# A decoder layer on one core: weight remainders made by TensorE, and head norms by a ones matrix and GpSimd's power

## The chip, the core and the metric

The kernel runs on one core of a Trainium2 chip. The engines are TensorE (PE, with its weight loads shown apart as PEld), VectorE (DVE), ScalarE (ACT), GpSimd (POOL) and SyncE (SP, which here only issues DMAs). Each has its own instruction queue and works it off in order; they meet only in semaphores. The metric is the device time of one execution in microseconds, the median of the runs.

## What is computed

One decoder layer over 16 sequences of 128 tokens and 256 features, three stages, each added to its input and layer-normed:

```
q = (q@fq1.T + b) * (q@fq2.T + b)   # per head, 16 heads of 16; k alike; v = x@wv.T
o = causal (q k^T) v                # no softmax
o = o * rsqrt(mean(o*o, per head) + 1e-5) * norm_w ;  x = LN(x + o @ wo.T)
y = conv(x1 * ctx) * ctx ...        # long convolution, 8 x 8 channel pairs; x = LN(x + y)
W = LUT[4-bit code] * scale         # gate, up, down: 3 matrices of 256 x 2048
x = LN(x + (gelu(x@Wg.T) * (x@Wu.T)) @ Wd.T)
```

All tensors are fp32. The large products run as three passes of TensorE's faster fp32r type: high x low, low x high, high x high, where high is the value rounded to fp32r and low is the remainder (value minus high).

## The kernel before

The 16 sequences go in four groups (0 to 3) of four, 512 tokens each. Features lie on partitions, tokens along the columns. The feed-forward part (FFN) of a group runs in 16 slots; a slot is a `gate` product, an `up` product and the `down` product of the slot before. Attention and convolution of the next group are cut into stages, and up to three stages are put between the three products of each slot (`slots`, and `last_slots` for group 3). So the program is: preparation; attention and convolution of group 0 alone; then three times FFN of group g-1 together with attention and convolution of group g; then the FFN of group 3 alone. Between them stands a `turn`, which projects q, k and v of the next group. The order is written out by hand and is the same list for all engines: `schedule` calls each engine's function of a stage's name, so an engine that waits in a stage holds everything behind it in its own queue.

The stages that matter here, with the slot in which they stand: eight `score` stages (slots 0 to 3; PE makes q k^T, DVE multiplies by the causal mask at L755, PE multiplies by v), `squares` (slot 4; ACT squares o, L583), `sums` (slot 5; PE sums the squares of each head into 64 columns, L1163), `rms` (slot 5; DVE, eleven small operations of 64 columns each, Newton steps for the reciprocal root, L769 to L786), `wide` (slot 6; ACT spreads 64 to 1024 columns, L589), `factor` (slot 7; PE transposes them, L1177, ACT copies them to SBUF, L596, DVE multiplies o by them, L793), `outproj` (slot 8; PE, L1187), `norm` (slot 9).

In group 0, where no FFN runs beside, the FFN weights are unpacked in 24 pieces of 512 columns: SP fetches codes and scales into one of two buffers, DVE shifts (L718), masks (L729) and scales (L733) them to `weight`, ACT rounds that to `ffn_hi` (L539), and two pieces later DVE subtracts for `ffn_lo` (L724). One piece stands beside each `score` stage. PE has little to do there and runs filler products (`keep_busy`, L1077), eight in each score stage. The last nine pieces go beside the slots of group 1, one each in slots 1 to 9 (`SECOND`).

GpSimd, which has no access to PSUM, makes the pair products of the convolution (L486) and the reciprocal roots of the layer norms as a power of -0.5 over two columns (L436).

Of the kernel before, what the change touches and what calls it, by code (L numbers as in the profile page):

```python
# [20 lines left out]
P = 128  # L21
# [11 lines left out]
NQ = F // QC  # L33
NTOEP = 4
NU_S = KT * NB
LN_EPS = 1e-5
# [16 lines left out]
def decoder_layer(nc, x, xT, ctx, ctxT, wq, wk, wvT, woT, fT, bias, skip, toep,  # L53
# [7 lines left out]
    with ExitStack() as stack:  # L61
# [13 lines left out]
        toep_sb = sb("toep_sb", [P, NTOEP, 2 * P])  # L75
        ident = sb("ident", [P, P])
        causal = sb("causal", [P, P])
        head_one = sb("head_one", [P, HT, DK])
# [5 lines left out]
        skip_sb = sb("skip_sb", [P, 1])  # L84
        minus_half = sb("minus_half", [P, 1])

        with ExitStack() as early:
# [4 lines left out]
            inter = sbe("inter", [P, 2, T])  # L92
        wv_lo = sb("wv_lo", [P, KT, D], F32R)
        xT_lo = sb("xT_lo", [P, KT, T], F32R)
        inter_lo = sb("inter_lo", [P, 2, T], F32R)

        xT_hi = sb("xT_hi", [P, KT, T], F32R)
# [6 lines left out]
        conv_sb = gate_q[:].rearrange("p k (b t) -> p k b t", b=NB)  # L104
        qT_sb = sb("qT_sb", [P, KT, T])
        rms_sb = x1T_sb = qT_sb
# [36 lines left out]
        ffn_banks = psum[4:8]  # L143
        skip_ps = x2T_ps = psum[4:6]


        def sems(*names):
# [3 lines left out]
            "ld_fold", "ld_wo", "ld_factors", "ld_small", "ld_xT", "ld_x", "ld_ctxT", "ld_ctx", "stored")  # L151
        ld_w = sems("ld_w_even", "ld_w_odd")
        ld_toep = sems(*[f"ld_toep{i}" for i in range(NTOEP)])

# [16 lines left out]
            "ms_ready", "newton_step", "rms_ready", "half_ready", "sk_ready", "x2lo_ready", "inter_ready", "ilo_ready")  # L171
        shifted, masked, deq_ready, wlo_ready = sems("shifted", "masked", "deq_ready", "wlo_ready")

        y_ready, st_ready, mv_ready, ve_ready, ln_ready = (
# [6 lines left out]

        last_mm, last_stored = sems("last_mm", "last_stored")
        end_inter, end_hi, end_lo = sems("end_inter", "end_hi", "end_lo")
        rstd_ready = sems("rstd_ready1", "rstd_ready2", "rstd_ready3")


        raw_w = sb("raw_w", [P, 2, QC], I32)
        raw_s = sb("raw_s", [P, 2, QC])
        code = sb("code", [P, 2, QC], I32)
# [61 lines left out]

        SECOND = [(0, 1, 0) if 1 <= s <= 9 else (0, 0, 0) for s in range(NT)]
        START = 1
        FIRST = START + 4 + sum(with_piece(*stage) for slot in slots for stage in slot)
        UNITS_FIRST = FIRST + 2

        def is_last(g):
# [19 lines left out]
        def ahead(g):  # L277

            return g == 1

        def proj_bank(g, p):
# [71 lines left out]
        def _(sp):  # L353
# [24 lines left out]
            def fetch(u):  # L378
                m, c = units[u]
                codes, scales = packed[m]  # L380
                sp.dma_start(raw_w[:, u % 2, :], codes[:, c * QC:(c + 1) * QC]).then_inc(ld_w[u % 2], 16)
                src = scales[:, c * QC:(c + 1) * QC].unsqueeze(1).broadcast_to([HT, P // HT, QC])
                sp.dma_start(raw_s[:, u % 2, :], src).then_inc(ld_w[u % 2], 16)

            fetch(0)
            fetch(1)
            load(0)
            for u in range(2, len(units)):
# [4 lines left out]
                sp.wait_ge(deq_ready, u - 1)  # L393
                fetch(u)
# [13 lines left out]
        def _(pool):  # L408
# [4 lines left out]
            nc.gpsimd.memset(skip_mat[:], 1.0).then_inc(filled, 1)  # L413
            nc.gpsimd.memset(minus_half[:], -0.5).then_inc(filled, 1)
            nc.gpsimd.memset(v_sb[:], 0.0).then_inc(filled, 1)
            pool.wait_ge(filled, 6)
            masks = ((head_one, HT, DK), (skip_mat, CH, CI))
# [83 lines left out]
            def norm2(g, _):  # L501
                rstd(g, 1)

            schedule(pool, turn, {"score": score, "norm": norm, "norm2": norm2, "x1T": x1T, "conv": conv}, nothing, nothing, nothing, nothing,
                     lambda: rstd(G - 1, 2))
# [3 lines left out]
        def _(act):  # L509
# [11 lines left out]
            act.dma_start(wo_sb[:], woT.rearrange("(k p) n -> p k n", p=P)).then_inc(ld_wo, 16)  # L521

            for i in range(4):
# [7 lines left out]
            act.wait_ge(filled, 6)  # L531
            act.wait_ge(bd_ready, 1)

            def unpack(step):
# [140 lines left out]
        def _(dve):  # L675
# [34 lines left out]
            def unpack(n):  # L710
                if n < NU:


                    dve.wait_ge(ld_w[n % 2], 32 * (n // 2 + 1))
                    if n:
                        dve.wait_ge(deq_ready, n)
                    for w in range(2):
                        nc.vector.tensor_scalar(code[:, w], raw_w[:, n % 2], 28 - 4 * w, 3, ALU.logical_shift_left,  # L718
                                                ALU.arith_shift_right).then_inc(shifted, 1)
                q = n - 2  # L720
                if 0 <= q < NU:
                    m, c = units[q]
# [4 lines left out]
                if n < NU:  # L727
                    dve.wait_ge(shifted, 2 * n + 2)
                    nc.vector.tensor_scalar(code[:], code[:], -0x72000000, None, ALU.bitwise_and).then_inc(masked, 1)  # L729
                    if n >= 2:  # L730
                        dve.wait_ge(wlo_ready, n - 1)
                    dve.wait_ge(masked, n + 1)
                    nc.vector.scalar_tensor_tensor(weight[:, n % 2], code_f16, 2.0 ** 14,  # L733
                                                   raw_s[:, n % 2].unsqueeze(1).broadcast_to([P, 2, QC]),
                                                   ALU.mult, ALU.mult).then_inc(deq_ready, 1)
# [321 lines left out]
        def _(pe):  # L1057
# [70 lines left out]
            def score(g, u):  # L1128
# [15 lines left out]
                if u < NU_S:  # L1144
# [10 lines left out]
                    last.then_inc(s_mm, 1)  # L1155
                keep_busy(g, 8 if u < NU_S else 4)

            def sums(g, mt):

                count(pe, sq_ready, 2, g, 2)  # L1160
                for b in range(NB):
# [3 lines left out]
                last.then_inc(ms_mm, 1)  # L1165
                if mt == KT - 1 and ahead(g + 1):
                    for p in range(3):
                        proj(g + 1, p)

            def factor(g, _):  # L1170

                count(pe, wide_ready, 1, g, 1)
                wide = rms_sb[:].rearrange("p k t -> p (k t)")
# [115 lines left out]
            def weights_ready(g, n, m):  # L1289

                if isinstance(g, int) and g == 0 and n % 2 == 0:
                    pe.wait_ge(wlo_ready, 3 * (n // 2) + m)

# [102 lines left out]
```

## Time and profile before

| | |
|---|---|
| median of 3 runs | 555.57 us (554.32 to 555.93) |
| the profiled execution's own time | 556.13 us |
| its span, first to last instruction | 553.8 us |
| PE busy | 529.0 us (96%) |
| DVE busy | 373.8 us (67%) |
| ACT busy | 147.3 us (27%) |
| POOL busy | 124.4 us (22%) |
| mean granted TensorE clock | 0.991 of full |

The busy time of PE counts the filler products too, and its ends are modelled, so whether PE is the limit of a stretch is read from its gaps and from what it waits for. The stretches of the span: preparation and group 0 to 113 us (its scores from 28.4 to 54.5 us), then FFN of group 0 with group 1 to 238.7 us, FFN of group 1 with group 2 to 363.4 us, FFN of group 2 with group 3 to 474 us, FFN of group 3 alone to the end.

### The profile page before, as it was taken

To read this page: it belongs to the slowest core of one execution; us is meant where nothing else is said; L and a number is where in the kernel's file an instruction comes from. 1 tells how busy PE (TensorE), PEld (TensorE's weight loads), DVE (VectorE), ACT (ScalarE), POOL (GpSimd) and SP (SyncE) were. 2 spreads that over 40 slices of the span, in tenths; PEclk is the share of its full clock that TensorE was granted. 3 is DMA by queue.
4 is the path that set the end of the run, shared out by engine and by line. 5 is a ranking of instruction groups with operands and counts; after the bars stand their busy time and mean duration, and the time that the engine had idled before them with its cause. 6 is when DMAs were issued, how large, how long until landed. Compare 5 with 4: busy or idle time off the path is not lost.

```text
span 553.8 us, 8791 instructions
## 1 busy us (share of the span) xinstructions
PE 529.0 (96%) x3351; PEld 430.9 (78%) x3351; DVE 373.8 (67%) x784; ACT 147.3 (27%) x260; POOL 124.4 (22%) x195
## 2 busy tenths in 40 slices
PE   4999889989989999999999999999999999999994
PEld 4766777657878888776888888776888888888883
DVE  3899879967767586975455586976455677753235
ACT  3432320052333112142242112141232111332221
POOL 2100059400002445030002445030003561010001
PEclk9999989989999999999999999999999999999998
DMA  6432223121210110013001111022001120010001
GB/s 190 150 113 80 89 69 96 38 77 40 62 35 30 48 49 29 1 63 130 1 0 30 48 48 30 1 64 92 0 1 44 53 59 0 1 38 2 1 0 38
DMA packets 25257, 26.81 MB, mean 48 GB/s; under 512 B 2816, under 2 KB 22784, under 8 KB 25216
## 3 DMA queue, kind: packets, MB, share of 16 engines
q1 hardware_dynamic: 14208, 15.73, 9.3%
q10 hardware_dynamic: 10576, 8.95, 5.5%
q0 software_dynamic: 432, 1.57, 0.8%
q8 instruction: 26, 0.43, 0.3%
q14 instruction: 15, 0.12, 0.1%
HBM read 24.15 MB, written 2.10 MB: 47 GB/s over the span
## 4 chain that ended last, share of the span: by engine, by line
PE 84%; DVE 8%; DMA 3%; issue 2%; POOL 1%; ACT 1%; ACTq 0%; POOLq 0%; SPq 0%; DVEq 0%
PE bank L1083 17%; PE bank L1085 16%; PE bank L1084 16%; PE front_bank L1215 5%; PE front_bank L1218 5%; PE front_bank L1216 5%; PE front_bank L1152 4%; PE front_bank L1139 3%; PE bank L1077 3%; PE front_bank L1083 2%; PE front_bank L1084 2%; PE front_bank L1085 2%; PE front_bank L1187 2%; DMA wo_sb<-in_woT 1%; PE front_bank L1163 1%
## 5 line engine op out<-in xcount | busy, mean ns | idle before, releaser
L1083 PE MATMUL bank<-x2T_lo,ffn_hi 128*128 128x512 f32 x256 | 110.6, 432 | 1.4 <-DVE x2T_lo L970 1.4
L1027 DVE TENSOR_TENSOR inter<-bank,inter 128x512 f32<-128x512 f32 x63 | 43.5, 690 | 86.1 <-PE bank L1085 85.7
L1085 PE MATMUL bank<-x2T_hi,ffn_hi 128*128 128x512 f32 x256 | 101.6, 397 | 0.0
L1084 PE MATMUL bank<-x2T_hi,ffn_lo 128*128 128x512 f32 x256 | 101.5, 396 | 0.0
L486 POOL TENSOR_TENSOR qbd<-qT_sb,ctxT_sb 128x256 f32<-128x256 f32 x128 | 79.2, 642 | 70.3 <-PE front_bank L1218 56.9
L436 POOL TENSOR_TENSOR ve<-ve,minus_half 128x2 f32<-128x2 f32 x24 | 17.1, 729 | 289.5 <-DVE ve L810 230.5
L667 ACT ACTIVATE inter_hi<-inter 128x512 fp32r<-128x512 f32 x63 | 39.8, 632 | 143.3 <-DVE inter L1027 143.3
L1083 PE MATMUL bank<-ffn_lo,inter_hi 128*128 128x256 f32 x256 | 76.7, 300 | 0.4 <-DVE inter_lo L1008 0.2
L654 ACT ACTIVATE inter<-bank 128x512 f32<-128x512 f32 x64 | 38.2, 598 | 133.7 <-PE bank L1085 133.6
L1085 PE MATMUL bank<-ffn_hi,inter_hi 128*128 128x256 f32 x256 | 71.9, 281 | 0.0
L1084 PE MATMUL bank<-ffn_hi,inter_lo 128*128 128x256 f32 x256 | 71.9, 281 | 0.0
L1016 DVE TENSOR_TENSOR inter_lo<-inter,inter_hi 128x512 fp32r<-128x512 f32 x63 | 47.5, 753 | 23.2 <-PE bank L1085 15.4
L1083 PEld LDWEIGHTS bank<-x2T_lo,ffn_hi 128*128 128x128 f32 x256 | 48.3, 189 | 16.3 <-issue 8.0
L1085 PEld LDWEIGHTS bank<-x2T_hi,ffn_hi 128*128 128x128 f32 x256 | 48.4, 189 | 11.8
L1084 PEld LDWEIGHTS bank<-x2T_hi,ffn_lo 128*128 128x128 f32 x256 | 48.3, 189 | 8.3 <-issue 0.2
L755 DVE TENSOR_TENSOR gate_q<-front_bank,causal 128x1024 f32<-128x1024 f32 x32 | 39.1, 1223 | 21.9 <-PE front_bank L1152 21.9
L1083 PEld LDWEIGHTS bank<-ffn_lo,inter_hi 128*128 128x128 f32 x256 | 48.2, 188 | 5.3 <-issue 3.0
L847 DVE TENSOR_TENSOR qbd<-front_bank,ctxT_sb 128x256 f32<-128x256 f32 x128 | 47.8, 415 | 5.0 <-PE front_bank L1218 4.6
L1084 PEld LDWEIGHTS bank<-ffn_hi,inter_lo 128*128 128x128 f32 x256 | 48.4, 189 | 1.8
L1085 PEld LDWEIGHTS bank<-ffn_hi,inter_hi 128*128 128x128 f32 x256 | 48.2, 188 | 0.0
L852 DVE TENSOR_REDUCE gate_q<-qbd 128x64 f32<-128x512 f32 x64 | 43.9, 686 | 2.2
L1215 PE MATMUL front_bank<-qbd,toep_sb 128*128 128x256 f32 x128 | 39.9, 393 | 2.7 <-POOL qbd L486 1.9
(130 smaller groups left out, 778.9 us busy)
## 6 DMA issues: line engine op xcount, KB each, us to landing
toep_sb<-in_toep ACTq DMA_DIRECT2D x64, 128.0 KB, 2.1
xT_sb<-in_xT SPq DMA_DIRECT2D x4, 512.0 KB, 5.0
ctxT_sb<-in_ctxT SPq DMA_DIRECT2D x4, 512.0 KB, 4.9
x_sb<-in_x SPq DMA_DIRECT2D x4, 512.0 KB, 6.0
ctx_sb<-in_ctx SPq DMA_DIRECT2D x4, 512.0 KB, 6.9
out<-ctxT_sb POOLq DMA_DIRECT2D x3, 512.0 KB, 3.4
raw_w<-in_gate_p SPq DMA_DIRECT2D x8, 128.0 KB
raw_s<-in_gate_s SPq DMA_DIRECT2D x8, 128.0 KB
```

The lines of the kernel that those rows point to most:

```text
L486: nc.gpsimd.tensor_tensor(pairs(kv_sb, h % 2)[:, kt], v_i, c_j, ALU.mult).then_inc(kv_ready, 1)
L654: nc.scalar.activation(inter[:, n % 2, :], gate_ps[:, :], ACT.Gelu_apprx_tanh).then_inc(gelu_ready, 1)
L667: nc.scalar.activation(inter_hi[:, n % 2, :], inter[:, n % 2, :], ACT.Copy).then_inc(ihi_ready, 1)
L755: nc.vector.tensor_tensor(sc_sb.rearrange("p (r k) c -> p r k c", k=2), front_ps[:, :, 0:2 * P].rearrange("p r (k c) -> p r k c", c=P), ca ...
L847: last = nc.vector.tensor_tensor(pairs(z_sb, h % 2)[:, lt], fb[h % 2][:, :].rearrange("p (k b j i) -> p k b j i", k=KT, b=NB, i=CI)[:, lt] ...
L852: nc.vector.tensor_reduce(conv_sb[:, :, :, h * CI:(h + 1) * CI], pairs(z_sb, h % 2), AX.X, ALU.add)\
L1016: nc.vector.tensor_tensor(inter_lo[:, n % 2, :], inter[:, n % 2, :], inter_hi[:, n % 2, :].bitcast(F32), ALU.subtract).then_inc(ilo_ready, 1)
L1027: nc.vector.tensor_tensor(inter[:, n % 2, :], up_ps[:, :], inter[:, n % 2, :], ALU.mult).then_inc(inter_ready, 1)
L1083: nc.tensor.matmul(ps, w_hi, x_lo, start=start, stop=False, skip_group_check=True)
L1084: nc.tensor.matmul(ps, w_lo, x_hi, start=False, stop=False, skip_group_check=True)
L1085: return nc.tensor.matmul(ps, w_hi, x_hi, start=False, stop=stop, skip_group_check=True)
L1215: nc.tensor.matmul(fb[h % 2][:, 0:n], diag, kv[:, 0:n], start=True, stop=True)
```

## The change

Six edits. First, in group 0's eight score stages the remainder `ffn_lo` of one piece (pieces 4 to 11) is made by PE and ACT and not by DVE: PE multiplies `weight` by the identity in plain fp32, runs one filler, and adds `ffn_hi` times minus the identity into the same PSUM bank; ACT copies the bank to `ffn_lo`. This stands in the place of the eight fillers. Second, the piece beside slot 6 of group 1 goes to slot 10. Third, a Gelu activation of one column early in ACT's queue. Fourth, three buffers for the fetched codes and scales, and so three fetches before SP's first other loads. Fifth, in groups 1 to 3 the head norms are made in another way: ACT rounds the squares to a high part, DVE makes the low part, PE multiplies both by a block matrix of ones (16 x 16 blocks), so that each feature's row holds its head's sum, ACT multiplies by 1/16 and adds 1e-5 on the way to `fac_sb`, and GpSimd raises 2 x 512 columns of it to the power -0.5. DVE's eleven operations, ACT's spreading and copies and PE's transposes of these groups go. Sixth, PE's projections of group 1 during `sums` of group 0 wait for ACT's last copy.

```
-        SECOND = [(0, 1, 0) if 1 <= s <= 9 else (0, 0, 0) for s in range(NT)]
+        SECOND = [(0, 1, 0) if 1 <= s <= 10 and s != 6 else (0, 0, 0) for s in range(NT)]
+        def low_on_pe(q):
+            return FIRST_SCORE <= q + 1 < FIRST_SCORE + NU_S
+        def by_block(g):
+            return g > 0
...
-            fetch(0)
-            fetch(1)
+            for u in range(NRAW):
+                fetch(u)
...
+            def wide(g, _):          # POOL
+                if by_block(g):
+                    for mt in range(KT):
+                        count(pool, mean_ready, 2, g - 1, mt + 1)
+                        nc.gpsimd.tensor_tensor(fac_sb[:, mt, :], fac_sb[:, mt, :],
+                                                minus_half[:].broadcast_to([P, T]), ALU.pow).then_inc(fac_ready, 1)
...
+                    if low_on_pe(n):          # ACT, unpack
+                        act.wait_ge(wlo_mm, n + 2 - FIRST_SCORE)
+                        nc.scalar.activation(ffn_lo[:, m, :, c * QC:(c + 1) * QC],
+                                             low_ps[n % 2][:, :].rearrange("p (w n) -> p w n", w=2), ACT.Copy)\
+                            .then_inc(wlo_act, 1)
...
+                if by_block(g):          # ACT, squares
+                    count(act, sq_ready, 2, g, mt + 1)
+                    if mt == 0:
+                        count(act, v_mm, 2, g, 2)
+                    nc.scalar.activation(sq_hi[:, mt, :], rms_sb[:, mt, :], ACT.Copy).then_inc(sqhi_ready, 1)
...
+                if by_block(g):          # ACT, wide
+                    for mt in range(KT):
+                        nc.scalar.activation(by_seq(fac_sb, mt), factor_part(mt), ACT.Identity, scale=1.0 / DK,
+                                             bias=rms_eps[:, 0:1]).then_inc(mean_ready, 1)
+                    return
...
-                if 0 <= q < NU:          # DVE, unpack
+                if 0 <= q < NU and not low_on_pe(q):
...
+                if by_block(g):          # DVE, squares
+                    count(dve, sqhi_ready, 2, g - 1, mt + 1)
+                    nc.vector.tensor_tensor(sq_lo[:, mt, :], rms_sb[:, mt, :], sq_hi[:, mt, :].bitcast(F32),
+                                            ALU.subtract).then_inc(sqlo_ready, 1)
...
-                count(dve, rT_ready, 2, g, 2)          # DVE, factor
+                if by_block(g):
+                    count(dve, fac_ready, 2, g - 1, 2)
+                else:
+                    count(dve, rT_ready, 2, g, 2)
...
-                keep_busy(g, 8 if u < NU_S else 4)          # PE, score
+                if g == 0 and u < NU_S:
+                    low_part(FIRST_SCORE + u - 1)
+                else:
+                    keep_busy(g, 4)
+            def low_part(q):
+                m, c = units[q]
+                pe.wait_ge(deq_ready, q + 1)
+                if q == FIRST_SCORE - 1:
+                    pe.wait_ge(minus_ready, 1)
+                if q >= FIRST_SCORE + 1:
+                    pe.wait_ge(wlo_act, q - FIRST_SCORE)
+                bank = low_ps[q % 2][:, :]
+                nc.tensor.matmul(bank, ident[:], weight[:, q % 2].rearrange("p w n -> p (w n)"),
+                                 start=True, stop=False, skip_group_check=True)
+                keep_busy(0, 1)
+                pe.wait_ge(whi_ready, q + 1)
+                nc.tensor.matmul(bank.rearrange("p (w n) -> p w n", w=2), minus_ident[:],
+                                 ffn_hi[:, m, :, c * QC:(c + 1) * QC], start=False, stop=True,
+                                 skip_group_check=True).then_inc(wlo_mm, 1)
...
+                if by_block(g):          # PE, sums
+                    if g == 1 and mt == 0:
+                        pe.wait_ge(block_ready, 1)
+                    count(pe, sqlo_ready, 2, g - 1, 2)
+                    for b in (2 * mt, 2 * mt + 1):
+                        toks = slice(b * S, (b + 1) * S)
+                        out = fb[b][:, 0:2 * S].rearrange("p (m t) -> p m t", m=KT)
+                        nc.tensor.matmul(out, head_block[:], sq_hi[:, :, toks], start=True, stop=False)
+                        last = nc.tensor.matmul(out, head_block[:], sq_lo[:, :, toks], start=False, stop=True)
+                    last.then_inc(ms_mm, 1)
+                    return
...
+            def factor(g, _):          # PE and ACT
+                if by_block(g):
+                    return
```

PE in group 0, two score stages, before (L1152 is q k^T, L1077 the filler, L1139 the product with v):

```order
L1152 MATMUL front_bank<-qbd,kT_sb 128x256 x4
L1077 MATMUL bank<-fold_hi 128x512 x8
L1139 MATMUL front_bank<-gate_q,v_sb 32x128 x8
L1152 MATMUL front_bank<-qbd,kT_sb 128x256 x4
L1077 MATMUL bank<-fold_hi 128x512 x8
```

The same place in the changed program (L1243 and L1247 are the two identity products):

```order
L1224 MATMUL front_bank<-qbd,kT_sb 128x256 x4
L1243 MATMUL bank<-weight,ident 128x512
L1149 MATMUL bank<-fold_hi 128x512
L1247 MATMUL bank<-ffn_hi,minus_ident 128x512
L1211 MATMUL front_bank<-gate_q,v_sb 32x128 x8
L1224 MATMUL front_bank<-qbd,kT_sb 128x256 x4
```

Seven of the eight fillers of each stage are gone, and one is left between the two identity products.

GpSimd from the end of group 0 to the norm of group 1, before (L442 spreads q for the scores):

```order
L436 TENSOR_TENSOR ve<-ve,minus_half 128x2 x2
L442 TENSOR_TENSOR qbd<-qT_sb,half_sel 128x256 x4
L436 TENSOR_TENSOR ve<-ve,minus_half 128x2 x2
L486 TENSOR_TENSOR qbd<-qT_sb,ctxT_sb 128x256 x28
```

And in the changed program:

```order
L465 TENSOR_TENSOR ve<-ve,minus_half 128x2 x2
L471 TENSOR_TENSOR qbd<-qT_sb,half_sel 128x256 x4
L485 TENSOR_TENSOR kT_sb<-kT_sb,minus_half 128x512 x2
L465 TENSOR_TENSOR ve<-ve,minus_half 128x2 x2
L522 TENSOR_TENSOR qbd<-qT_sb,ctxT_sb 128x256 x28
```

Two powers of 512 columns (`fac_sb` is the tile kT_sb) have come in between the scores and the first norm.

PE in slot 5 of the FFN of group 1, with `sums` of group 2, before:

```order
L1163 MATMUL front_bank<-head_sel,qT_sb 128x8 x4
L1083 MATMUL bank<-x2T_lo,ffn_hi 128x512
L1084 MATMUL bank<-x2T_hi,ffn_lo 128x512
L1085 MATMUL bank<-x2T_hi,ffn_hi 128x512
```

And in the changed program (the tile of the high part is that of xT_hi):

```order
L1261 MATMUL front_bank<-xT_hi,head_block 128x256
L1262 MATMUL front_bank<-sq_lo,head_block 128x256
L1261 MATMUL front_bank<-xT_hi,head_block 128x256
L1262 MATMUL front_bank<-sq_lo,head_block 128x256
L1155 MATMUL bank<-x2T_lo,ffn_hi 128x512
```

Four sums of eight columns have become four of 256 columns, of which two need DVE's low part.

## Rows read from the trace of the kernel before

**Rows 1.** The page: busy us, share of the span and instructions.
```profile
PE 529.0 (96%) x3351; PEld 430.9 (78%) x3351; DVE 373.8 (67%) x784; ACT 147.3 (27%) x260; POOL 124.4 (22%) x195
```

**Rows 2.** Windows: us; PE, PEld, DVE, ACT, POOL busy (count); clock; DMA share; GB/s.
```profile
28.40:54.50 26.10, 26.06 (x257) 16.94 (x257) 24.80 (x48) 6.64 (x14) 1.23 (x2) 1.00 0.34 98
...
113.00:150.00 37.00, 36.89 (x325) 26.21 (x325) 28.06 (x47) 14.81 (x29) 1.53 (x2) 0.95 0.17 54
...
238.70:363.40 124.70, 124.70 (x815) 102.91 (x814) 80.28 (x163) 32.16 (x57) 30.03 (x45) 1.00 0.13 39
```

**Rows 3.** Groups by line and shape, GpSimd: busy us, mean ns, idle before.
```profile
L436 POOL TENSOR_TENSOR ve<-ve,minus_half 128x2 f32<-128x2 f32 x24 | 17.1, 729 | 289.5 <-DVE ve L810 230.5 <-DVE ve L1045 59.0
L463 POOL TENSOR_TENSOR kT_sb<-x_sb,ctx_sb 128x512 f32<-128x512 f32 x8 | 11.1, 1388 | 0.0
L414 POOL MEMSET minus_half<- 128x1 f32 x1 | 0.1, 89 | 0.0
```

**Rows 4.** Line L436 alone: count, shortest, median and longest ns.
```profile
L436 POOL TENSOR_TENSOR ve<-ve,minus_half x24: 690/692/912, 72.5 to 549.6; 128x2 f32<-128x2 f32 x24
```

**Rows 5.** Timeline of group 0's scores, DVE: start, us, engine, line.
```profile
49.08 1.22 DVE L755 TENSOR_TENSOR gate_q<-front_bank,causal 128x1024 f32<-128x1024 f32 x1
...
50.62 0.68 DVE L724 TENSOR_TENSOR ffn_lo<-weight,ffn_hi 128x512 fp32r<-128x512 f32 x1
...
51.22 0.42 DVE L729 TENSOR_SCALAR code<-code 128x512 int32<-128x512 int32 x1
...
52.35 1.22 DVE L755 TENSOR_TENSOR gate_q<-front_bank,causal 128x1024 f32<-128x1024 f32 x1
```

**Rows 6.** The chain of waits: start, us, what; group 0's scores, then group 2.
```profile
47.46 0.57 PE front_bank L1139 x16
48.04 0.64 PE front_bank L1152 x8
48.68 2.04 PE bank L1077 x8
...
289.20 1.73 PE front_bank L1187 x8
...
348.13 1.72 PE bank L1226 x4
```

**Rows 7.** Timeline of group 0's output projection, DVE.
```profile
66.99 0.50 DVE L718 TENSOR_SCALAR code<-raw_w 128x256 int32<-128x256 int32 x2 [0.54 <-DMA raw_s<-in_gate_s]
...
69.14 0.68 DVE L827 TENSOR_TENSOR x_sb<-front_bank,x_sb 128x512 f32<-128x512 f32 x1
```

**Rows 8.** Timeline of group 2's head norm, ACT, PE and DVE.
```profile
270.92 0.28 PE L1083 MATMUL bank<-ffn_lo,inter_hi 128*128 128x256 f32 x1
271.28 0.28 PE L1083 MATMUL bank<-ffn_lo,inter_hi 128*128 128x256 f32 x1
...
272.38 1.07 ACT L583 ACTIVATE qT_sb<-front_bank 128x512 f32<-128x512 f32 x2
...
273.74 0.95 PE L1163 MATMUL front_bank<-head_sel,qT_sb 128*128 128x8 f32 x8
274.55 0.47 PE L1083 MATMUL bank<-x2T_lo,ffn_hi 128*128 128x512 f32 x1
...
282.60 1.04 ACT L589 ACTIVATE qT_sb<-inv_rms 128x1024 f32<-128x1024 f32 x1
283.95 1.03 PE L1177 MATMUL front_bank<-ident,qT_sb 128*128 128x128 f32 x8
284.74 0.48 PE L1083 MATMUL bank<-x2T_lo,ffn_hi 128*128 128x512 f32 x1
...
286.21 1.29 DVE L793 TENSOR_TENSOR gate_q<-front_bank,kT_sb 128x512 f32<-128x512 f32 x2 [2.79 <-ACT kT_sb L596]
```

**Rows 9.** Timeline of group 1's transposes, PE.
```profile
159.21 1.09 PE L1177 MATMUL front_bank<-ident,qT_sb 128*128 128x128 f32 x8 [1.53 <-ACT qT_sb L589]
```

**Rows 10.** Timeline of the preparation, DVE.
```profile
9.86 0.48 DVE L697 TENSOR_SCALAR wo_sb<-wo_sb,b_small 128x512 f32<-128x512 f32 x1 [2.21 <-DMA wo_sb<-in_woT]
```

More of the change, by code:

```diff
@@ L34 @@
 NTOEP = 4
+NRAW = 3
 NU_S = KT * NB
@@ L76, in decoder_layer @@
         ident = sb("ident", [P, P])
+        minus_ident = sb("minus_ident", [P, P], F32R)
         causal = sb("causal", [P, P])
@@ L85, in decoder_layer @@
         minus_half = sb("minus_half", [P, 1])
+        rms_eps = sb("rms_eps", [P, 1])
+        head_block = sb("head_block", [P, P], F32R)
+        warm = sb("warm", [P, 1])
         with ExitStack() as early:
@@ L92, in decoder_layer @@
             inter = sbe("inter", [P, 2, T])
+            qT_sb = sbe("qT_sb", [P, KT, T])
         wv_lo = sb("wv_lo", [P, KT, D], F32R)
@@ L95, in decoder_layer @@
         inter_lo = sb("inter_lo", [P, 2, T], F32R)
+        sq_lo = sb("sq_lo", [P, KT, T], F32R)
         xT_hi = sb("xT_hi", [P, KT, T], F32R)
@@ L104, in decoder_layer @@
         conv_sb = gate_q[:].rearrange("p k (b t) -> p k b t", b=NB)
-        qT_sb = sb("qT_sb", [P, KT, T])
+        sq_hi = xT_hi
         rms_sb = x1T_sb = qT_sb
@@ L143, in decoder_layer @@
         ffn_banks = psum[4:8]
-        skip_ps = x2T_ps = psum[4:6]
+        skip_ps = x2T_ps = low_ps = psum[4:6]
         def sems(*names):
@@ L151, in decoder_layer @@
             "ld_fold", "ld_wo", "ld_factors", "ld_small", "ld_xT", "ld_x", "ld_ctxT", "ld_ctx", "stored")
-        ld_w = sems("ld_w_even", "ld_w_odd")
+        ld_w = sems(*[f"ld_w{i}" for i in range(NRAW)])
         ld_toep = sems(*[f"ld_toep{i}" for i in range(NTOEP)])
@@ L172, in decoder_layer @@
         shifted, masked, deq_ready, wlo_ready = sems("shifted", "masked", "deq_ready", "wlo_ready")
+        minus_ready, wlo_mm, wlo_act = sems("minus_ready", "wlo_mm", "wlo_act")
         y_ready, st_ready, mv_ready, ve_ready, ln_ready = (
@@ L182, in decoder_layer @@
         last_mm, last_stored = sems("last_mm", "last_stored")
+        block_ready, sqhi_ready, sqlo_ready, mean_ready, fac_ready = sems(
+            "block_ready", "sqhi_ready", "sqlo_ready", "mean_ready", "fac_ready")
         end_inter, end_hi, end_lo = sems("end_inter", "end_hi", "end_lo")
         rstd_ready = sems("rstd_ready1", "rstd_ready2", "rstd_ready3")
-        raw_w = sb("raw_w", [P, 2, QC], I32)
-        raw_s = sb("raw_s", [P, 2, QC])
+        raw_w = sb("raw_w", [P, NRAW, QC], I32)
+        raw_s = sb("raw_s", [P, NRAW, QC])
         code = sb("code", [P, 2, QC], I32)
@@ L255, in decoder_layer, with low_parts @@
         UNITS_FIRST = FIRST + 2
+        FIRST_SCORE = START + 4
+        def low_on_pe(q):
+            return FIRST_SCORE <= q + 1 < FIRST_SCORE + NU_S
+        def low_parts(eng, k):
+            beside_scores = sum(low_on_pe(q) for q in range(k))
+            if k > beside_scores:
+                eng.wait_ge(wlo_ready, k - beside_scores)
+            if beside_scores:
+                eng.wait_ge(wlo_act, beside_scores)
         def is_last(g):
@@ L380, in fetch @@
                 codes, scales = packed[m]
-                sp.dma_start(raw_w[:, u % 2, :], codes[:, c * QC:(c + 1) * QC]).then_inc(ld_w[u % 2], 16)
+                sp.dma_start(raw_w[:, u % NRAW, :], codes[:, c * QC:(c + 1) * QC]).then_inc(ld_w[u % NRAW], 16)
                 src = scales[:, c * QC:(c + 1) * QC].unsqueeze(1).broadcast_to([HT, P // HT, QC])
-                sp.dma_start(raw_s[:, u % 2, :], src).then_inc(ld_w[u % 2], 16)
-            fetch(0)
-            fetch(1)
+                sp.dma_start(raw_s[:, u % NRAW, :], src).then_inc(ld_w[u % NRAW], 16)
+            for u in range(NRAW):
+                fetch(u)
             load(0)
-            for u in range(2, len(units)):
+            for u in range(NRAW, len(units)):
                 if u == START + 4 + NU_S // 2:
@@ L392, in _ @@
                     load(1)
-                sp.wait_ge(deq_ready, u - 1)
+                sp.wait_ge(deq_ready, u - NRAW + 1)
                 fetch(u)
@@ L414, in _ @@
             nc.gpsimd.memset(minus_half[:], -0.5).then_inc(filled, 1)
+            nc.gpsimd.memset(rms_eps[:], RMS_EPS).then_inc(filled, 1)
             nc.gpsimd.memset(v_sb[:], 0.0).then_inc(filled, 1)
-            pool.wait_ge(filled, 6)
+            pool.wait_ge(filled, 7)
             masks = ((head_one, HT, DK), (skip_mat, CH, CI))
@@ L502, in norm2 @@
                 rstd(g, 1)
-            schedule(pool, turn, {"score": score, "norm": norm, "norm2": norm2, "x1T": x1T, "conv": conv}, nothing, nothing, nothing, nothing,
+            schedule(pool, turn, {"score": score, "wide": wide, "norm": norm, "norm2": norm2, "x1T": x1T, "conv": conv}, nothing, nothing, nothing, nothing,
                      lambda: rstd(G - 1, 2))
@@ L521, in _ @@
             act.dma_start(wo_sb[:], woT.rearrange("(k p) n -> p k n", p=P)).then_inc(ld_wo, 16)
+            act.wait_ge(filled, 7)
+            nc.scalar.activation(warm[:], minus_half[:], ACT.Gelu_apprx_tanh)
             for i in range(4):
@@ L530, in _ @@
             nc.scalar.activation(wv_hi[:], wv_sb[:], ACT.Copy).then_inc(wvhi_ready, 1)
-            act.wait_ge(filled, 6)
             act.wait_ge(bd_ready, 1)
+            act.wait_ge(const_ready, 4)
+            nc.scalar.activation(head_block[:], head_one[:].rearrange("p h e -> p (h e)"), ACT.Copy)\
+                .then_inc(block_ready, 1)
+            act.wait_ge(const_ready, 4)
+            nc.scalar.activation(minus_ident[:], ident[:], ACT.Copy, scale=-1.0).then_inc(minus_ready, 1)
             def unpack(step):
@@ L711, in unpack @@
                 if n < NU:
-                    dve.wait_ge(ld_w[n % 2], 32 * (n // 2 + 1))
+                    dve.wait_ge(ld_w[n % NRAW], 32 * (n // NRAW + 1))
                     if n:
@@ L730, in unpack @@
                     if n >= 2:
-                        dve.wait_ge(wlo_ready, n - 1)
+                        if low_on_pe(q):
+                            dve.wait_ge(wlo_mm, q + 2 - FIRST_SCORE)
+                        else:
+                            low_parts(dve, n - 1)
                     dve.wait_ge(masked, n + 1)
                     nc.vector.scalar_tensor_tensor(weight[:, n % 2], code_f16, 2.0 ** 14,
-                                                   raw_s[:, n % 2].unsqueeze(1).broadcast_to([P, 2, QC]),
+                                                   raw_s[:, n % NRAW].unsqueeze(1).broadcast_to([P, 2, QC]),
                                                    ALU.mult, ALU.mult).then_inc(deq_ready, 1)
@@ L1155, in score @@
                     last.then_inc(s_mm, 1)
-                keep_busy(g, 8 if u < NU_S else 4)
-            def sums(g, mt):
+                if g == 0 and u < NU_S:
+                    low_part(FIRST_SCORE + u - 1)
+                else:
+                    keep_busy(g, 4)
[14 more added lines that the diff above has]
+                                 skip_group_check=True).then_inc(wlo_mm, 1)
+            def sums(g, mt):
+                if by_block(g):
+                    if g == 1 and mt == 0:
[7 more added lines that the diff above has]
+                    last.then_inc(ms_mm, 1)
+                    return
                 count(pe, sq_ready, 2, g, 2)
@@ L1166, in sums @@
                 if mt == KT - 1 and ahead(g + 1):
+                    pe.wait_ge(wlo_act, NU_S)
                     for p in range(3):
@@ L1170, in factor @@
             def factor(g, _):
+                if by_block(g):
+                    return
                 count(pe, wide_ready, 1, g, 1)
@@ L1291, in weights_ready @@
                 if isinstance(g, int) and g == 0 and n % 2 == 0:
-                    pe.wait_ge(wlo_ready, 3 * (n // 2) + m)
+                    low_parts(pe, 3 * (n // 2) + m)
             def down(g, n, pair_done=None):
```

2 lines of the change are left out of this document (1 added, 1 removed).

## The prediction

> **What bounds the kernel now.** The page comes first: PE is busy for 529 of 553.8 us [rows 1]. The windows then say where that is real. Where FFN and another group run together PE has no gap: in the 124.7 us of the FFN of group 1 it is busy for all of them, while DVE has a third free and POOL three quarters [rows 2]. There, time is PE work, and any new wait of PE is lost in full. In group 0's scores PE is just as busy (26.06 of 26.1 us) [rows 2], but the chain of waits shows 2.04 us of each step going to eight fillers [rows 6], so the limit is elsewhere: on the timeline DVE goes from one mask (49.08) to the next (52.35) without a gap, 3.27 us a step [rows 5]. What matters for the fifth edit is POOL: its only power is over two columns, and it takes 692 ns in the median, with little spread (690 to 912) [rows 4].
>
> All is summed against the profiled execution's own time, 556.13 us (span 553.8 and 2.3 around it), which is 0.56 us above the median of the runs.
>
> **The scores of group 0.** DVE loses the subtraction L724 from each step, 0.60 us from its start to that of the next operation (50.62 to 51.22) [rows 5]: 2.67 us remain. PE's new step is 0.57 (product with v) + 0.64 (q k^T) [rows 6] + the identity product in fp32 + one filler + the second identity product. A 512-column fp32 product costs 1.72 / 2 = 0.86 us (two products of skips, each recorded as two passes) [rows 6]; a filler and the fp32r pass 2.04 / 8 = 0.255 us each. Sum 2.58. The low part waits for `weight`, which DVE finishes as its step ends, and the next mask waits for the q k^T behind it, so the loop passes through both engines: 2.58 and about 0.1 of handing over, 2.7 us. ACT gains one copy of about 0.6 us a step and has the room (6.64 us busy of 26.1) [rows 2]. The first of the eight steps still has the subtraction, so seven shrink by 0.57: **-4.0 us**. Bounds: 0 (if the pass through PE, ACT and PSUM costs as much as it saves) and -4.8 (eight times 0.60).
>
> **The rest of group 0.** One more piece, that beside `rms`, loses its 0.60 us on DVE, and the third buffer takes away a wait of 0.54 us for scales before `outproj` [rows 7], both in front of DVE's addition at 69.14: **-1.0 us** (0 to -1.14). The early Gelu takes a table load out of slot 0, where PE hardly waits at all (36.89 us busy of 37 from 113 on) [rows 2]: 0. The wait of group 1's projections for ACT's last copy: ACT's squares stand behind that copy anyway, 0. The third fetch goes out while `wo` is still arriving, for which DVE waits 2.21 us [rows 10]: **+0.3** (0 to +1).
>
> **Groups 1 to 3, without the power.** In each, PE loses two sums of 0.81 us (273.74 to 274.55) and the transposes, 0.79 us (283.95 to 284.74), and gains eight passes of 256 columns at 0.36 / 3 = 0.12 us (270.92 to 271.28: three such passes), 0.96 us [rows 8]: 1.45 less, **-4.3** in three groups. In group 1 a wait of 1.53 us before the transposes goes too [rows 9]: **-1.5**. DVE's eleven small operations go, but it wasn't late there: 0. Against this stands a new wait: PE's `sums` need ACT's two roundings and DVE's last subtraction. ACT ended the squares at 273.45, 0.29 us before PE wanted them (273.74) [rows 8]. Two more ACT passes of about 0.6 us and one of DVE of 0.65 come in: 1.9 less 0.3 is a wait of 1.6 us each, **+4.8** (bounds +3.3, if the passes overlap, and +6).
>
> Without the power this is -4.0 - 1.0 + 0.3 - 4.3 - 1.5 + 4.8 = **-5.7 us**.
>
> **The power.** Two instructions of 512 columns in each of three groups. What hides them: ACT's work at 282.60 becomes two copies of 0.55, so POOL can start at about 283.25. PE wants `outproj` at 289.20 [rows 6], 0.79 earlier without the transposes, and DVE needs 1.29 us for the factor before [rows 8]: POOL must be done by 287.0. So 3.7 us a group are free; the rest is a wait of DVE, with `inner` of the FFN queued behind it, and so of PE: from `outproj` and the next `up` on PE has nothing that it may do. Nor can the conv stages go ahead, since POOL makes their products behind the powers.
>
> No row has a power of more than two columns, so the price per column is the question.
> - From above: 346 ns, the row of two columns taken as all per column (692 / 2): 354 us a group.
> - From below: 2.7 ns, as POOL's multiplication of 512 columns (1388 ns) [rows 3], with the 692 - 89 = 603 ns of the short power as a cost of each instruction: 2 x (1.39 + 0.60) = 4.0 us a group.
>
> I take it near the upper row: the smallest POOL instruction, a memset of one column, shows that an instruction as such costs about 89 ns [rows 3]; nothing in the trace suggests that a power sets up for longer than a multiplication, so 603 ns belong to two columns, 301 each. 1024 x 0.301 + 0.2 = 309 us a group, of which 3.7 are hidden: 3 x 305.3 = **+916 us**. After each such stand PE may start at the low one of its two clock levels (1.2 and not 2.4 GHz). The one fall inside a full stretch that the rows show is that of 113 to 150 us, granted 0.95 [rows 2], 1.85 us lost: three times, **+5.5**. Forecast: 556.1 - 5.7 + 916 + 5.5 - 0.6 = **1471 us**.
>
> The Trainium skill speaks against so high a price (GPSIMD Engine Reference, Performance versus the Vector engine, and Performance pitfalls): a chain of dependent fp32 operations costs 4 cycles each on that engine, but a loop whose elements are independent is bound by issue, at about 3 operations a cycle, so a short instruction shows the chain and a long one the rate. An estimate by that page: 603 ns are 724 cycles at its 1.2 GHz, 362 a column, some 90 chained operations, at 3 a cycle 30 cycles or 25 ns a column; 26 us a group, and 556.1 - 5.7 + 3 x (25.8 - 3.7) + 5.5 - 0.6 = 622 us. No row shows whether the loop is written so; that is the third line of case 2.
>
> **The cases.** A change within 0.3% (1.7 us) can't be told from none here.
> 1. *Price by the column, 270 to 346 ns* (46%): 1471 us, own range 1370 to 1625. For it: the short power is dear and constant. Against it: there is only one width.
> 2. *Price by blocks of columns or overlapped, 15 to 270 ns* (33%). If the 603 ns pay for a block of four, 151 ns a column, 154 us a group (12%): 555.3 + 3 x 150.7 = 1007 us. A block of eight, 77 us a group (11%): 775 us.
>    If the columns overlap, so that most of 603 ns is the way of one column through the loop, and the pace is that of ten multiplications (10 x 2.7 = 27 ns, 28 us a group; 10%): 555.3 + 3 x 24 = 627 us. For it: two columns are fewer than a loop would take at once. Against it: nothing in the rows.
> 3. *The power is hidden* (17%, of which 14% faster, 3% no change). A fixed cost of 0.6 us per instruction and the pace of a multiplication, 4.0 us against 3.7 free: 556.1 - 5.7 + 0.9 - 0.6 = 551 us, faster. It is the other side, and decides as long as a column costs under about 5 ns, where the wait eats the 5.7 us. For it: POOL has its time free and the 603 ns could be a set-up. Against it: 600 ns of set-up would be seven times the shortest instruction.
> 4. *A few ns a column, 5 to 15* (4%): 552 to 585 us, the gain of the rest lost.
>
> That the first four edits don't do what they say, because PE in the scores waits on the way through ACT, moves every case by up to 5 us and decides only between 3 and no change.
>
> Faster 14%, no change 3%, slower 83%. The range 580 to 1630 us holds cases 1 and 2 and leaves out case 3 and most of case 4; the likeliest case alone spans 1370 to 1625.
>
> **What will show it.** The duration of the two powers of 128x512 in groups 1 to 3: about 154 us each if right, under 2.5 us in case 3. DVE's `factor` waiting for POOL for nearly that pair, PE's windows in slots 7 and 8 empty, and a lower granted clock after them. A score step of 2.7 us for 3.26; PE waiting about 1.6 us for `sq_lo` in each of the three groups; no wait for scales before `outproj` of group 0. I am wrong above all if the power's cost isn't in proportion to its columns; everything else is worth 6 us.

## The result, and the profile after

The changed kernel takes 1040.26 us (median of 4 runs, 1039.70 to 1040.98) against 555.18 us before: a ratio of 1.874 [1.871, 1.877]. It is slower, as forecast, but by 485 us and not by 915.

The page of the changed kernel, busy time of each engine and the shares of its chain of waits by engine, beside [rows 1]:

```profile
PE 529.4 (51%) x3271; PEld 426.1 (41%) x3271; DVE 365.9 (35%) x746; ACT 152.3 (15%) x273; POOL 616.7 (59%) x202
...
POOL 48%; PE 43%; DVE 4%; issue 2%; ACT 1%; DMA 1%; ACTq 0%; POOLq 0%; DVEq 0%
```

PE's busy time is what it was, 529 us, but its share fell from 96 to 51%. POOL has gained 492 us, and POOL makes 48% of the chain. The line that answers to [rows 4] is the power of 512 columns (the changed kernel, that line alone, durations shortest/median/longest in ns):

```profile
L485 POOL TENSOR_TENSOR kT_sb<-kT_sb,minus_half x6: 81911/81920/81949, 155.3 to 808.3; 128x512 f32<-128x512 f32 x6
```

81.92 us an instruction, 160 ns a column, six times with hardly a spread. Who waits for it (the changed kernel's waits: us in total, times, longest):

```profile
DVE gate_q L865 <- POOL kT_sb L485: 491.6, 3, 163.9
...
PE front_bank L1295 <- DVE gate_q L865: 481.3, 4, 160.3
```

DVE stands at `factor` for the whole pair in each group, and PE behind it in `outproj`, 160.3 us at most: of each pair of 163.8 us, 3.6 were hidden (the working had 3.7). The timeline of group 1 in the changed kernel answers to [rows 8], which is of group 2: the roundings and subtractions ahead of `sums`, then the power, `factor` and `outproj`:

```profile
143.74 0.63 ACT L628 ACTIVATE xT_hi<-qT_sb 128x512 fp32r<-128x512 f32 x1
...
144.89 0.63 ACT L628 ACTIVATE xT_hi<-qT_sb 128x512 fp32r<-128x512 f32 x1
...
145.61 0.68 DVE L827 TENSOR_TENSOR sq_lo<-qT_sb,xT_hi 128x512 fp32r<-128x512 f32 x1
...
146.44 0.36 PE L1261 MATMUL front_bank<-xT_hi,head_block 128*128 128x256 f32 x1 [1.79 <-DVE sq_lo L827]
...
155.31 81.93 POOL L485 TENSOR_TENSOR kT_sb<-kT_sb,minus_half 128x512 f32<-128x512 f32 x1 [31.71 <-ACT kT_sb L643]
...
319.23 1.29 DVE L865 TENSOR_TENSOR gate_q<-front_bank,kT_sb 128x512 f32<-128x512 f32 x2 [163.84 <-POOL kT_sb L485]
...
320.57 3.78 PE L1295 MATMUL front_bank<-wo_sb,gate_q 128*128 128x256 f32 x8 [160.26 <-DVE gate_q L865]
323.80 0.99 PE L1155 MATMUL bank<-x2T_lo,ffn_hi 128*128 128x512 f32 x1
```

The new wait of PE for the low parts is there, 1.79 us. In the long wait for the powers the granted clock is 0.52, and after it PE starts at its low clock (granted 0.50, 1.2 GHz): the eight passes of `outproj` take 3.23 us (320.57 to 323.80) where they took 1.73 [rows 6] (windows of the changed kernel; columns as in [rows 2]):

```profile
157.60:319.00 161.40, 2.71 (x18) 2.10 (x16) 0.00 (x0) 0.00 (x0) 161.40 (x2) 0.52 0.00 0
320.57:323.80 3.23, 3.23 (x9) 2.60 (x9) 2.58 (x6) 0.48 (x1) 0.00 (x0) 0.50 0.00 0
```

In group 0 the masks of the score stages, which answer to [rows 5], now alternate between steps of 3.01 and 2.81 us, 2.91 in the mean (the changed kernel's timeline):

```profile
38.79 1.22 DVE L818 TENSOR_TENSOR gate_q<-front_bank,causal 128x1024 f32<-128x1024 f32 x1
...
41.80 1.23 DVE L818 TENSOR_TENSOR gate_q<-front_bank,causal 128x1024 f32<-128x1024 f32 x1
...
44.61 1.22 DVE L818 TENSOR_TENSOR gate_q<-front_bank,causal 128x1024 f32<-128x1024 f32 x1
```

The chain of waits of the same stretch (columns as in [rows 6]; L1243 and L1247 are the identity products, L1149 the filler, L1211 the product with v, L1224 q k^T) goes once through PE and once through DVE in two such steps: 2.87 us from the identity product to the mask (38.93 to 41.80) and 2.95 from the mask to the identity product of the next weight (to 44.75).

```profile
38.93 1.12 PE bank L1243 x2
40.05 0.23 PE bank L1149
40.28 0.23 PE bank L1247
40.52 0.57 PE front_bank L1211 x16
41.09 0.69 PE front_bank L1224 x8
...
41.80 0.04 DVE gate_q L818
...
44.00 0.70 DVE weight L796
...
44.75 1.12 PE bank L1243 x2
```

### The profile page after: what moved, and what is told of

The parts are those of the page before. It is cut to its first block, busy times and chain, and to the rows that moved or that the text cites. A ratio compares the mean times of both kernels' runs of the same rounds, so it can differ in the third digit from the quotient of the medians.

```text
span 1038.2 us, 8626 instructions
## 1 busy us (share of the span) xinstructions
PE 529.4 (51%) x3271; PEld 426.1 (41%) x3271; DVE 365.9 (35%) x746; ACT 152.3 (15%) x273; POOL 616.7 (59%) x202
## 4 chain that ended last, share of the span: by engine, by line
POOL 48%; PE 43%; DVE 4%; issue 2%; ACT 1%; DMA 1%; ACTq 0%; POOLq 0%; DVEq 0%
POOL kT_sb L485 47%; PE bank L1155 8%; PE bank L1156 8%; PE bank L1157 8%; PE front_bank L1323 3%; PE front_bank L1326 2%; PE front_bank L1324 2%; PE front_bank L1295 2%; PE front_bank L1224 2%; PE front_bank L1211 2%; PE front_bank L1155 1%; PE front_bank L1157 1%; PE front_bank L1156 1%; DMA wo_sb<-in_woT 1%; DVE inter L1099 0%
## 5 line engine op out<-in xcount | busy, mean ns | idle before, releaser
L485 POOL TENSOR_TENSOR kT_sb<-kT_sb,minus_half 128x512 f32<-128x512 f32 x6 | 491.5, 81927 | 91.4 <-ACT kT_sb L643 91.4
L1295 PE MATMUL front_bank<-wo_sb,gate_q 128*128 128x256 f32 x64 | 20.7, 483 | 481.3 <-DVE gate_q L865 481.3
L1295 PEld LDWEIGHTS front_bank<-wo_sb,gate_q 128*128 128x128 f32 x64 | 15.1, 242 | 485.8 <-DVE gate_q L865 483.1
L865 DVE TENSOR_TENSOR gate_q<-front_bank,kT_sb 128x512 f32<-128x512 f32 x8 | 5.2, 686 | 492.5 <-POOL kT_sb L485 491.6
```

The source lines that it names most:

```text
L485: nc.gpsimd.tensor_tensor(fac_sb[:, mt, :], fac_sb[:, mt, :], minus_half[:].broadcast_to([P, T]), ALU.pow).then_inc(fac_ready, 1)
L1295: last = nc.tensor.matmul(fb[j][:, (b % 2) * D:(b % 2 + 1) * D], o_sb[:, kt, b * S:(b + 1) * S], wo_sb[:, kt, :], start=kt == 0, stop=kt = ...
```

## The experiments

**The old norms.** The changed kernel without its fifth edit.

```
         def by_block(g):
-            return g > 0
+            return False
```

> The changed kernel with the old head norms in all groups: the identity products, the moved piece, the early Gelu and the third buffer alone. Theory (the power of 1024 columns is the whole loss): the first product of the FFN stood at 110.26 us in the changed kernel and at 113.11 before, and group 1's wait of 1.53 us before its transposes may go since the piece beside slot 6 is moved: 555.2 - 2.9 - 0 to 1.5 = 551 to 552.5 us, faster by 0.5 to 0.8%. Rival (something of these edits also costs in later groups): 555 us or more.

Measured: 550.75 us against 555.21, ratio 0.9919 [0.9902, 0.9936]. Edits one to four and six are a gain of 4.5 us; the whole loss is in the fifth. The transposes of group 1 no longer wait. Of the five edits, the moved piece, the third fetch and the identity products are tried further below; the early Gelu and the wait for ACT's last copy were not run by themselves.

**Times for power.** The same chain of instructions, with the dear operation exchanged for a cheap one (so the reciprocal root is left out of groups 1 to 3).

```
-                                                minus_half[:].broadcast_to([P, T]), ALU.pow).then_inc(fac_ready, 1)
+                                                minus_half[:].broadcast_to([P, T]), ALU.mult).then_inc(fac_ready, 1)
```

> The changed kernel with GpSimd multiplying the 2 x 512 columns by -0.5 in place of raising them to the power -0.5 (the reciprocal root is left out of groups 1 to 3). Theory: two multiplications of 1.39 us fit into the 3.7 us that were reckoned free, so no wait for GpSimd is left; against the kernel with the old norms PE has 4.3 us less work in three groups and waits 5.4 us (three times the 1.79 us seen) for the low parts of the squares: 552 to 553.5 us, within 0.3% of the kernel with the old norms. Rival 1 (the ones matrix is worth its 4.3 us, the wait for the low part overlaps with something): 547 to 549 us. Rival 2 (the free time is shorter than reckoned): 555 us or more, with DVE's factor still waiting for GpSimd.

Measured: 551.68 us, ratio 0.9945 [0.9924, 0.9966]. The price of this one operation, with the low clock that follows its waits, is the difference of 488.6 us between this kernel and the changed one. With the power at a multiplication's cost the fifth edit would still be worth nothing: 0.9 us above the old norms, intervals overlapping. Its work on PE is less, but the wait for the low parts takes the gain back (waits of PE in this kernel):

```profile
PE front_bank L1261 <- DVE sq_lo L827: 5.2, 3, 1.8
```

A multiplication of 512 columns by a broadcast column took 1.04 us, so the pair was hidden.

**Powers of 1 to 128 columns.** The kernel before with a row of scratch instructions ahead of everything.

```
...
+            for op, width in [(ALU.pow, w) for w in (1, 2, 3, 4, 5, 6, 8, 9, 12, 16, 32, 64, 128)] + \
+                             [(ALU.mult, w) for w in (1, 4, 64, 512)]:
+                pool.wait_ge(tried, n)
+                nc.gpsimd.tensor_tensor(power_sb[:, 0:width], base_sb[:, 0:width],
+                                        minus_half[:].broadcast_to([P, width]), op).then_inc(tried, 1)
...
+            nc.gpsimd.tensor_tensor(power_sb[0:16, 0:48], base_sb[0:16, 0:48],
+                                    minus_half[0:16].broadcast_to([16, 48]), ALU.pow).then_inc(tried, 1)
```

> The kernel before, with a row of powers of -0.5 on GpSimd ahead of everything, of 1 to 128 columns, and multiplications of 1, 4, 64 and 512 columns. The power took 692 ns for 2 columns and 81.92 us for 512, which is 160.0 ns a column. Theory A (columns are worked off in fours, about 640 ns a block): 1 to 4 columns 690 ns each, 5, 6 and 8 1330 ns, 9 and 12 1970 ns, 64 columns 10.3 us, 128 columns 20.5 us. Theory B (a set-up of some 370 ns and 160 ns for every column): 1, 2, 3, 4 columns 530, 690, 850, 1010 ns, 8 columns 1650 ns, 64 columns 10.6 us. Theory C (301 ns for each of the first columns, cheaper later): 4 columns about 1290 ns. The time of the kernel is of no use here; it grows by some 55 us.

Groups by line and shape (busy us, mean ns of one); the second one of 128x1 and the one of 128x512 are multiplications, the others powers:

```profile
L438 POOL TENSOR_TENSOR power_sb<-base_sb,minus_half 128x1 f32<-128x1 f32 x1 | 0.7, 666 | 0.1
L438 POOL TENSOR_TENSOR power_sb<-base_sb,minus_half 128x2 f32<-128x2 f32 x1 | 0.7, 706 | 0.1
L438 POOL TENSOR_TENSOR power_sb<-base_sb,minus_half 128x3 f32<-128x3 f32 x1 | 0.9, 877 | 0.1
L438 POOL TENSOR_TENSOR power_sb<-base_sb,minus_half 128x4 f32<-128x4 f32 x1 | 1.0, 1008 | 0.1
L438 POOL TENSOR_TENSOR power_sb<-base_sb,minus_half 128x5 f32<-128x5 f32 x1 | 1.2, 1167 | 0.1
L438 POOL TENSOR_TENSOR power_sb<-base_sb,minus_half 128x8 f32<-128x8 f32 x1 | 1.6, 1635 | 0.1
...
L438 POOL TENSOR_TENSOR power_sb<-base_sb,minus_half 128x128 f32<-128x128 f32 x1 | 20.7, 20727 | 0.1
...
L438 POOL TENSOR_TENSOR power_sb<-base_sb,minus_half 128x1 f32<-128x1 f32 x1 | 0.2, 191 | 0.1
L438 POOL TENSOR_TENSOR power_sb<-base_sb,minus_half 128x512 f32<-128x512 f32 x1 | 1.0, 1042 | 0.1
...
L442 POOL TENSOR_TENSOR power_sb<-base_sb,minus_half 16x48 f32<-16x48 f32 x1 | 8.0, 7986 | 0.1
```

Theory A falls: 3 and 4 columns cost more than 2. Theory B holds from 2 columns on: through 692 ns for 2 and 81920 for 512 columns goes a line of 373 ns and 159.3 ns a column, and it gives 1647 ns for 8 (1635 measured) and 20.76 us for 128 (20.73). One column misses: 666 ns for the 530 of the theory; it was the first power of the run, and whether that or the width is the reason was not tried. In this run the widths of 9 to 64 lay 0.2 to 0.5 us above the line; why was not tried either (64 columns in the next kernel lie on it). All bases here are 2.0, in the changed kernel they are means of squares, and one line fits both; the exponent was -0.5 throughout.

**A power of 64 columns.** The old norms, with the reciprocal root of the 64 distinct head sums on GpSimd in groups 1 to 3.

```
+            def rms(g, _):          # POOL
+                if g > 0:
+                    count(pool, ms_ready, 1, g, 1)
+                    count(pool, wide_ready, 1, g, 0)
+                    nc.gpsimd.tensor_tensor(inv_rms[:], mean_sq[:], minus_half[:].broadcast_to([P, NB * H]),
+                                            ALU.pow).then_inc(rms_ready, 1)
...
```

> The kernel with the old norms, but in groups 1 to 3 the reciprocal root of the 64 head sums is one power of 64 columns on GpSimd in place of DVE's ten Newton steps. Theory (160 ns for each column, whatever the width): 10.3 us a group, from 278.5 to 288.8 us in the place of group 2, where the transposes of PE were due at 283.95 and ACT spreads 1.1 us before: PE waits about 6 us in each group, +18 us, 569 to 572 us. Rival (mostly a set-up, 0.7 to 2 us for 64 columns): hidden, as the kernel with the old norms.

Measured: 576.69 us (572.79 to 578.38), ratio 1.0378 [1.0344, 1.0412], some 5 us above the theory's 569 to 572; the mechanism is as expected. Line and waits of this kernel:

```profile
L485 POOL TENSOR_TENSOR inv_rms<-mean_sq,minus_half x3: 10527/10542/10543, 149.2 to 411.5; 128x64 f32<-128x64 f32 x3
...
PE front_bank L1296 <- ACT qT_sb L654: 18.3, 3, 6.1
```

10.54 us is on the line (10.57), and PE waits 6.1 us in each group. 18.3 us of the 25.9 above the old norms are this wait. Most of the other 7.6 is the low clock after it (window from the transposes of group 1 on, columns as in [rows 2]):

```profile
160.88:165.90 5.02, 5.02 (x18) 4.44 (x19) 1.82 (x5) 2.04 (x4) 0.00 (x0) 0.51 0.01 3
```

From the transposes to `outproj` PE took 7.41, 7.32 and 7.63 us in the three groups and 5.10 with the old norms, which makes 7.1 us more in all.

**The piece put back.** The old norms, with `SECOND` as before.

```
-        SECOND = [(0, 1, 0) if 1 <= s <= 10 and s != 6 else (0, 0, 0) for s in range(NT)]
+        SECOND = [(0, 1, 0) if 1 <= s <= 9 else (0, 0, 0) for s in range(NT)]
```

> The kernel with the old norms (550.75 us), with the moved piece put back beside slot 6 of group 1. Theory: it was this piece, and not the Newton steps, that made PE wait 1.53 us before the transposes of group 1, since the old norms no longer have that wait with the piece moved: about 552.2 us, with a wait of about 1.5 us before the transposes of group 1. Rival (the wait went for another reason, as the third buffer): 550.8 us, no wait.

Measured: 551.46 us, ratio 0.9930 [0.9911, 0.9947]; the interval overlaps that of the old norms. The trace decides: the wait of [rows 9] is back (timeline):

```profile
155.27 1.09 PE L1285 MATMUL front_bank<-ident,qT_sb 128*128 128x128 f32 x8 [1.52 <-ACT qT_sb L647]
```

**The third fetch later.**

```
-            for u in range(NRAW):
+            for u in range(2):
                 fetch(u)
             load(0)
+            fetch(2)
```

> The kernel with the old norms, with the third fetch of codes and scales issued behind SP's first other loads and not ahead of them. Theory: the third fetch shares the DMA engines with wo, for which DVE waits at the start (wo landed 1.1 us later than before in the changed kernel, and the scores began 0.5 us later): 0.3 to 0.6 us faster, 550.2 to 550.5 us, wo again about 7 us under way. Rival (the early Gelu or the longer preparation of constants delays the start): 550.7 us, the scores begin as late as before.

Measured: 550.43 us, ratio 0.9909 [0.9891, 0.9927], not to be told from the old norms. `wo` was under way for 7.43 us here, 7.21 with the old norms and 8.11 in the changed kernel, which issue the same DMAs ahead of it; before it was 6.97. Single profiles scatter as widely as the effect sought, so whether the third fetch delays the start stays open.

**No filler.** The old norms, without `keep_busy(0, 1)` in `low_part`.

> The kernel with the old norms, without the one filler between the two identity products. Theory: the score steps of 2.91 us are set by a loop through DVE and PE (weight, identity products, product with v, q k^T, mask, weight), so 0.25 us less on PE shortens each of seven steps until DVE's own 2.67 us are met: -1.6 us, about 549.2 us. Rival (the filler lies in the time in which the second identity product waits for ACT's rounding): no change, 550.7 us. A lower granted clock in or after the scores would speak for the filler.

Measured: 549.42 us, ratio 0.9900 [0.9877, 0.9923]; the steps are 2.80 us, not the 2.67 expected, and DVE has no gap in them. The expectation of -1.6 us is met with -1.3, but the interval overlaps that of the old norms; that the steps fell is the trace's word.

**The older piece.** Each score stage makes the low part of the piece one older.

```
         def low_on_pe(q):
-            return FIRST_SCORE <= q + 1 < FIRST_SCORE + NU_S
+            return FIRST_SCORE <= q + 2 < FIRST_SCORE + NU_S
...
-                    low_part(FIRST_SCORE + u - 1)
+                    low_part(FIRST_SCORE + u - 2)
...
```

> The kernel with the old norms, where each score stage makes the low part of the piece one older (pieces 3 to 10 for 4 to 11): its weight is finished a whole step before PE wants it. Theory: the wait for the weight is what ties PE to DVE, so without it the step falls from 2.91 us to DVE's own 2.67 us or PE's 2.6: seven steps of 0.24, -1.7 us; one piece less of DVE's work is saved behind the scores and one more ahead of them: about 549 us. Rival (the handing over is somewhere else, as from q k^T to the mask): 550.7 us and steps of 2.9 us.

Measured: 549.19 us, ratio 0.9889 [0.9871, 0.9908], the lowest median of all. The steps are 2.79 us, and DVE has no gap in them (timeline of one step):

```profile
37.61 1.22 DVE L820 TENSOR_TENSOR gate_q<-front_bank,causal 128x1024 f32<-128x1024 f32 x1
38.74 0.49 DVE L780 TENSOR_SCALAR code<-raw_w 128x256 int32<-128x256 int32 x2
39.26 0.43 DVE L791 TENSOR_SCALAR code<-code 128x512 int32<-128x512 int32 x1
39.80 0.69 DVE L798 SCALAR_TENSOR_TENSOR weight<-code,raw_s 128x512 f32<-128x512 f16 x1
40.40 1.22 DVE L820 TENSOR_TENSOR gate_q<-front_bank,causal 128x1024 f32<-128x1024 f32 x1
```

So DVE's own step is 2.79 and not 2.67 us: the shift, which now stands right before the operation that needs it (which waits for the shift's semaphore), takes 0.52 to the next start (38.74 to 39.26) and not 0.41, as it did before the subtraction at 50.62 [rows 5] (the kernel before):

```profile
50.21 0.48 DVE L718 TENSOR_SCALAR code<-raw_w 128x256 int32<-128x256 int32 x2
```

**All three.** The older piece, the later fetch, no filler.

> The kernel with the old norms, with all three: the low part of the piece one older, no filler between the identity products, and the third fetch behind SP's first other loads. Theory: with the older piece the score step is DVE's own 2.79 us (mask 1.13, shift 0.52, and 0.53, scale 0.61), so the missing filler gives nothing more there (PE waits instead), and the late fetch moved nothing that can be told from the scatter of wo's arrival (7.0 to 8.1 us over all runs): as the kernel with the older piece, 549 us. Rival (PE's and DVE's steps are so near each other that the filler still counts): 547.5 to 548.5 us and steps under 2.79 us.

Measured: 549.45 us, ratio 0.9899 [0.9881, 0.9918], steps of 2.80 us: nothing beyond the older piece, as the theory said.

## Why the prediction was right, and what it mis-sized

**The bound and the wait: right.** That a power off PE would stop PE, through `factor` on DVE, at `outproj`, came as worked out: 3.6 us of each pair hidden for 3.7 in the working, and 480.8 us of waiting in three groups (the 481.3 above hold 0.5 of group 0). That there is no other work for PE in the meantime is seen in its window.

**The price per column: wrong, 301 ns for 159.3.** The step that failed is "603 ns belong to two columns": the memset of 89 ns was taken for all that an instruction costs as such. The run of the widths shows a line with 373 ns beside the columns, and a multiplication of one column, which would have been the fitting row and wasn't there, takes 191 ns. Measured, the term "+916" is 3 x (163.8 - 3.6) = +481. The likeliest case was so put too high; the outcome lies in the second case, near its first line (151 ns a column, 1007 us), and by another mechanism than that line named: not a block of four, but a set-up. That the line came so near is luck; that the range held the outcome is not, since it was drawn to cover prices of this size. One width can't part a set-up from a slope, which was said, but the slope was taken near its upper end.

By the rule of the Trainium skill (GPSIMD Engine Reference, Performance versus the Vector engine) that a loop of three or more operations an element is bound by issue, at roughly 3 operations a cycle, the estimate was 25 ns a column and 622 us. The measurement decides: 159.3 ns. What the same page of the Trainium skill says of the layout (Architecture), that each of the eight cores works on its own 16 partitions, agrees with the run of the widths: 48 columns on 16 partitions took 7.99 us, and the line for 128 partitions gives 8.02.

**The clock after the stand: a little low.** 1.85 us each was put in. From the first half of `outproj` to its second it took 5.65, 5.11 and 5.17 us after the three stands and 3.12 with the old norms (158.95 to 162.07), so 2.5, 2.0 and 2.1 were lost, at granted clocks of 0.56 to 0.64.

**The scores of group 0: -4.0 predicted, -2.4 measured.** From the first mask to the eighth it took 23.14 us before (29.21 to 52.35) and 20.75 in the changed kernel (29.68 to 50.43). Two terms were mis-sized: DVE's own step (2.79 and not 2.67, since the subtraction had covered a wait of DVE for its own shift) and PE's passes in the loop: 2.84 us in the chain shown above and not 2.58, above all 1.12 for the first identity product where 0.86 was put in. Without the filler, or with the older piece, which takes the loop apart, the step falls to DVE's own 2.80 or 2.79.

**The rest of group 0: right.** From the eighth mask to the first product of the FFN it took 60.76 us before (52.35 to 113.11) and 59.83 in the changed kernel (50.43 to 110.26), -0.9 for -1.0. The scores began 0.5 us later, for +0.3; but the old norms with the same loads began them at 28.79, so this can't be put down to the third fetch.

**The wait of 1.53 us in group 1: right in size, wrong in place.** It was booked to the norms; the run with the piece put back shows that the moved piece removed it.

**Groups 1 to 3 without the power: right.** Less work of 4.3 us against waits of 4.8 was the sum; the waits measured 5.2, and the run with times for power came out even with the old norms. In all, "-5.7 us" without the power was -3.5 (551.68 against 555.21), the missing 2.2 being mostly the scores' 1.6.

## What to carry to other kernels

A price per element can't be read from one short instruction: find or make a second width before a wide one is put on the path, for one row fits a set-up and a slope alike, and between the two lay everything from 551 to 1600 us. Before an operation is moved to an idle engine, count the columns that it really needs: here the 1024 columns held what 64 columns hold in the old norms, each value sixteen times, and even these 64 cost 10.5 us and a wait, where eleven small operations of DVE had been hidden beside PE. And where PE has no gap, a new wait in its queue can eat as much as the work taken off it.

## What was not expected of the hardware

GpSimd's power of -0.5 costs 373 ns and 159.3 ns a column from 2 columns on, the same on 16 as on 128 partitions, while a multiplication of 512 columns by a broadcast one took 1.04 us: a ratio of 79. And where an operation of DVE waits by a semaphore for the one right before it, it starts some 0.11 us later than an independent one does in its place (0.52 for 0.41 us from start to start, behind the same shift).
